# Four edits to an AdaLN, attention and LoRA-MoE kernel: rsqrt by single columns, set-up order, turned logits, order of the last downs

## What is computed

```
mod = silu(c) @ wmod -> sa, ca, ga, sb, cb, gb (one row of 256 each per batch; |ga|, |gb| at least 0.25)
h = layernorm(x) * (1 + ca) + sa
x = x + ga * (attention(layernorm(h) * gamma + beta) @ o_proj + h)      causal, one head of 256
h = layernorm(x) * (1 + cb) + sb
x = x + gb * (base FFN(h) + sum over the top 2 of 8 experts of the LoRA FFN(h) by weight)
```

## Time and profile before

| | us |
|---|---|
| runs: median (lowest to highest of 3) | 670.13 (669.81 to 670.28) |
| the profiled execution, its own time | 669.96 |
| its span, first to last instruction | 668.1 |
| busy: PE | 652.1 (98%) |
| busy: PE weight load | 561.4 (84%) |
| busy: DVE | 466.5 (70%) |
| busy: POOL | 369.5 (55%) |
| busy: ACT | 360.3 (54%) |

### The profile page before, as it was taken

One profiled execution on the slowest core, in us unless ns is written; L12 is line 12 of the kernel. 1 busy time (PEld: TensorE's weight loads), 2 busy tenths in 40 slices (PEclk: granted clock), 3 DMA queues, 4 the chain that ended last, 5 costly groups with the idle time before them and its releaser, 6 DMA issues.

```text
span 668.1 us, 10913 instructions
## 1 busy us (share of the span) xinstructions
PE 652.1 (98%) x3890; PEld 561.4 (84%) x3890; DVE 466.5 (70%) x1146; ACT 360.3 (54%) x646; POOL 369.5 (55%) x442
## 2 busy tenths in 40 slices
PE   8799999999999999999999999999999999999996
PEld 6488987888889987888889897887889998798885
DVE  5857676888785776688776677689886757547323
ACT  1766466545555547555455446564455456654543
POOL 1099366538658236657676317665666525633644
PEclk9999999999999999999999999999999999999999
DMA  8400020000000020000000001000000000000000
GB/s 308 138 1 1 2 64 0 1 1 32 0 1 32 1 65 1 0 1 33 0 1 32 1 6 59 1 1 33 1 0 27 7 1 1 1 1 1 32 0 33
DMA packets 15032, 15.47 MB, mean 23 GB/s; under 512 B 1793, under 2 KB 13697, under 8 KB 14977
## 3 DMA queue, kind: packets, MB, share of 16 engines
q1 hardware_dynamic: 14976, 14.76, 6.6%
HBM read 10.57 MB, written 4.19 MB: 22 GB/s over the span
## 4 chain that ended last, share of the span: by engine, by line
PE 84%; DVE 10%; ACT 3%; issue 1%; DMA 1%; POOL 0%; SPq 0%; DVEq 0%; ACTq 0%
PE ps L1265 78%; PE ps L1274 6%; DVE hid L1112 2%; DVE rstd L844 1%; DVE zb L864 1%; DMA xs<-in_L_attn_x 1%; DVE neg_mean L1176 1%; ACT xr L587 1%; ACT act_s L725 1%; DVE zb L867 0%; DVE stat L998 0%; DVE stat L861 0%; DVE topi L1057 0%; DVE xr L1007 0%; DVE nr_a L842 0%
## 5 line engine op out<-in xcount | busy, mean ns | idle before, releaser
L475 POOL TENSOR_TENSOR ring_lo<-hid,ring_hi 128x512 fp32r<-128x512 f32 x144 | 187.2, 1304 | 110.0 <-ACT ring_hi L733 109.4
L725 ACT ACTIVATE act_s<-ps 128x512 f32<-128x512 f32 x120 | 71.6, 597 | 123.0 <-PE ps L1265 122.4
L1112 DVE TENSOR_TENSOR hid<-act_s,ps 128x512 f32<-128x512 f32 x120 | 82.1, 684 | 78.9 <-ACT act_s L725 74.1
L733 ACT ACTIVATE ring_hi<-hid 128x512 fp32r<-128x512 f32 (+1 forms) x144 | 90.4, 627 | 5.3 <-PE ps L1265 3.5
L1265 PE MATMUL ps<-wdT_hi,ring_hi 128*128 128x256 f32 x192 | 53.2, 283 | 0.0
L1265 PE MATMUL ps<-wdT_lo,ring_hi 128*128 128x256 f32 x192 | 52.7, 280 | 0.0
L467 POOL TENSOR_TENSOR xT_lo<-tr_full,xT_hi 128x512 fp32r<-128x512 f32 x28 | 35.9, 1297 | 29.0 <-ACT xT_hi L597 29.0
L1265 PE MATMUL ps<-wdT_hi,ring_lo 128*128 128x256 f32 x160 | 44.7, 280 | 0.0
L1265 PE MATMUL ps<-vv_hi,pT_hi 128*128 128x256 f32 x144 | 42.9, 298 | 0.1
L1265 PE MATMUL ps<-tm_hi,bgT_hi 128*128 128x512 f32 x96 | 39.5, 411 | 2.4 <-DVE hid L1112 2.4
L482 POOL TENSOR_TENSOR xr<-xr,y_gb 128x256 f32<-128x256 f32 x31 | 22.6, 754 | 33.6 <-DVE y_gb L1147 33.6
(11 more groups left out here) (232 smaller groups left out, 2018.2 us busy)
## 6 DMA issues: line engine op xcount, KB each, us to landing
out<-xr SPq DMA_DIRECT2D x7, 512.0 KB, 2.9
xs<-in_L_attn_x SPq DMA_DIRECT2D x3, 1024.0 KB, 5.7
xs<-in_L_attn_x SPq DMA_DIRECT2D x2, 512.0 KB, 4.7
s_mod<-in_L_wmod SPq DMA_DIRECT2D x2, 512.0 KB, 7.6
s_qkvT<-in_L_attn_qkv SPq DMA_DIRECT2D x1, 768.0 KB, 7.4
wgT_raw<-in_L_ffn_Wg SPq DMA_DIRECT2D x1, 704.0 KB, 7.9
wuT_raw<-in_L_ffn_Wu SPq DMA_DIRECT2D x1, 640.0 KB, 8.7
wdT_raw<-in_L_ffn_Wd SPq DMA_DIRECT2D x1, 640.0 KB, 5.7
```

Of the source, the lines that this page charges most:

```text
L475: pool.tensor_sub(ring[1][:, place(n), :], hid[:, n % HID, :], ring[0][:, place(n), :].bitcast(fp32)).then_inc(h_lo.sem, 1)
L725: nc.scalar.activation(act_s[:, n % 2, :], ps[:, 2 * (n % 2), :], ACT.Silu).then_inc(silu_ready.sem, 1)
L733: nc.scalar.activation(ring[0][p0:P, place(n), :], hid[p0:P, n % HID, :], ACT.Copy).then_inc(h_hi.sem, 1)
L1112: V.tensor_mul(hid[:, n % HID, :], act_s[:, n % 2, :], ps[:, 2 * (n % 2) + 1, :]).then_inc(h_ready.sem, 1)
```

## The change

1. **Rsqrt on single columns.** For layernorm 2 of tiles 4 to 7, `guess` and `rsqrt_steps` on [128, 4] become `single_guess` and `single_steps`: four instructions of one column each, all `tensor_scalar`, with the other factors as per-partition scalars. Statistics go from r = 4 to r = 2, the guess from r = 5 to r = 3, one step each at r = 4, 5, 6.
2. **Set-up with four tiles first.** Tiles 0 to 3 of batch 0 go ahead of tiles 4 to 7 on every engine; tiles 4 to 7's transposes, queries 2, 3, all values and two gate jobs move into attention steps i = 0 to 3. Scale jobs 1 to 3 are spread from one row by `batch_rows` (four partitions) in place of a product with the weight; a third `mod_row` makes that row. 28 dummy matmuls stand ahead of the first queries. ACT runs one small Exp early. All twelve `weight_high` go to i = 2 to 6; POOL's `weight_low` 7, 8 behind the Newton steps of layernorm 2, 9 to 11 behind the two `tr_low`.
3. **Second half's logits turned.** `logits(1)` becomes `logits_across`: four matmuls with Wr as weights and 512 columns of x moving, a DVE copy of the 16x512 result at r = 12, and `logits_back`: four transposes. `router_shift(1)` comes after the x_stats of r = 12; the next batch's moments and guess at r = 13, POOL's Newton steps at r = 14 to 16. `FILL` (0, 2) goes from 2, 2, 2, 1 to 0, 4, 2, 1.
4. **Last downs.** In the last batch the base's half tile (slot 0, a = 1) is the last of the six last downs.

Beside these: the mask banks of half 0 are 6, 7 instead of 7, 6, and each mask waits for its own x1 tile; in half 1 `ln1_stats` comes before `ln1_rows`.

```diff
+        mod_rows = wmask[0:B, :, :].rearrange("p s n -> p (s n)")
+        scale_rows = y_gb[0:B, :, :].rearrange("p t d -> p (t d)")
+        batch_rows = bc[0:B, B - 1, SA:CA + 1, :]...
+        gate_spread = bc[:, :, GA:GB + 1, :]...
...
+        LAST_DOWNS = ((0, 0), (1, 0), (1, 1), (2, 0), (2, 1), (0, 1))
-        MASK_BANKS = ((7, 6, 4, 5), (3, 4, 5, 6))
+        MASK_BANKS = ((6, 7, 4, 5), (3, 4, 5, 6))
-        EARLY_HIGH = 4
-        BODY_HIGH = {0: (4, 5, 6), 1: (7,), 2: (8,), 3: (9,), 4: (10,), 5: (11,)}
+        BODY_HIGH = {2: (0, 1), 3: (2, 3, 4), 4: (5, 6, 7), 5: (8, 9, 10), 6: (11,)}
-        MOD_BANKS = (0, 1, 2, 3, 7, 2, 3, 7)
+        MOD_JOBS = (("scale", 0), ("gate", 0), ("scale", 1), ("scale", 2), ("scale", 3), ("gate", 1), ("gate", 2), ("gate", 3))
+        MOD_BANKS = (0, 2, 6, 3, 4, 2, 7, 6)
+        ROW_CHUNKS = ((0, 1), (2, 5), (3, 4))
+        FIRST_PROJ = (0, 1, 4, 5, 2, 3, 6, 7)
+        W_ROUTER, W_UP = 6, 9
... POOL
                 for it in range(NEWTON):
                     newton(b, LN2_A, 0, TC, it)
+                if b == 0:
+                    for j in range(W_ROUTER + 1, W_UP):
+                        weight_low(j)
                 for k in range(KT):
                     tr_low(b, KT * NC + k, [t[:, 0, k, :] for t in xT])
+                if b == 0:
+                    for j in range(W_UP, WEIGHT_STEPS):
+                        weight_low(j)
... ACT
+            nc.scalar.activation(lg[:, 0, :], cT[...], ACT.Exp, scale=0.0).then_inc(unwaited, 1)
                 for i in range(NT):
+                    if b == 0 and i == 0:
+                        act.wait_ge(first_shift, 2)
+                        for tile in range(TC, NT):
+                            first_normalise(tile)
... DVE
+            def single_guess(tiles):
+                for i in tiles:
+                    mark(V.tensor_scalar(nr_v[:, i:i + 1], mv[:, i, 1:2], EPS, -0.5, ALU.add, ALU.mult))
+                settle()
+                for i in tiles:
+                    mark(V.tensor_scalar(nr_i[:, i:i + 1], nr_v[:, i:i + 1].bitcast(i32), 1, None, ALU.logical_shift_right))
+                settle()
+                for i in tiles:
+                    mark(V.tensor_scalar(rstd[:, i:i + 1].bitcast(i32), nr_i[:, i:i + 1], -1.0, float(0x5f3759df + 0x40000000 - 0x00400000), ALU.mult, ALU.add))
+                settle()
+            def single_steps(tiles):
+                for i in tiles:
+                    y = rstd[:, i:i + 1]
+                    mark(V.tensor_scalar(nr_a[:, i:i + 1], y, y, nr_v[:, i:i + 1], ALU.mult, ALU.mult))
+                settle()
+                for i in tiles:
+                    y = rstd[:, i:i + 1]
+                    mark(V.tensor_scalar(y, nr_a[:, i:i + 1], 1.5, y, ALU.add, ALU.mult))
+                settle()
...
-                    if r == 4:
+                    if r == 2:
                         x1_stats(TC + 3)
                         moments(range(TC, NT))
-                    if r == 5:
-                        mark(V.tensor_scalar(neg_mean[:, TC:NT], mv[:, TC:NT, 0], -1.0, None, ALU.mult))
-                        link(guess(TC, TC))
-                        rsqrt_steps(TC, TC, range(NEWTON - 1))
+                    if r == 3:
+                        single_guess(range(TC, NT))
+                    if 4 <= r < 4 + NEWTON:
+                        single_steps(range(TC, NT))
...
                     if r == 12:
-                        router_shift(1)
+                        dve.wait_ge(logits_wide.sem, logits_wide.at(b, 0))
+                        V.tensor_copy(logit_rows, ps[0:2 * E, LOGIT_BANK[1], :]).then_inc(logits_copied.sem, 1)
...
+                        if 3 <= r < 3 + NT:
+                            ln1_stats(r - 3)
                         if 2 <= r < 2 + NT:
                             ln1_rows(b + 1, r - 2)
-                        if 3 <= r < 3 + NT:
-                            ln1_stats(r - 3)
... PE, set-up
-                if what == "scale":
+                if job == 0:
                     for k in range(KT):
                         last_mm = mm(ps[:, bank, :], s_scb[:, k, b, :], s_mod[:, k, 0:2 * D], k == 0, k == KT - 1)
+                elif what == "scale":
+                    last_mm = mm(ps[:, bank, :], batch_rows[:, b, :], scale_rows, True, True)
...
+            attention_transposes(0, 0, [xr[:, i, :] for i in range(TC)])
+            mod_turned(1, modT_ready)
+            modulation(3)
+            pe.wait_ge(product_lo, 1)
+            modulation(4)
+            pe.wait_ge(mod_copied, 2)
+            for _ in range(28):
+                mm(ps[:, 2, 0:P], identb[:, :], identb[:, :], True, True)
+            queries(0, (0, 1))
+            pe.wait_ge(gates_spread, 2)
+            modulation(5)
... PE, attention of batch 0
+                        if b == 0 and i == 0:
+                            values(b, range(NT // 2))
+                        if b == 0 and i == 1:
+                            attention_transposes(b, 1, [xr[:, t, :] for t in range(TC, NT)])
+                            pe.wait_ge(modT_copied, 1)
+                            modulation(6)
+                            modulation(7)
+                        if b == 0 and i == 3:
+                            values(b, range(NT // 2, NT))
...
+                    if b == 0 and i == 2:
+                        queries(b, (2, 3))
... PE, FFN
+                def logits_across(ci):
+                    pe.wait_ge(tr_lo.sem, tr_lo.at(b, KT * NC + ci * KT + 1))
+                    o = ps[0:2 * E, LOGIT_BANK[ci], :]
+                    for k in range(KT):
+                        x_hi, x_lo = inputs(ci)[k]
+                        mm(o, wr_both[:, k, :, :].rearrange("p h e -> p (h e)"), x_hi, k == 0, False)
+                        last_mm = mm(o[0:E, :], wr_both[:, k, 0, :], x_lo, False, k == KT - 1)
+                    last_mm.then_inc(logits_wide.sem, 1)
+                def logits_back(ci):
+                    pe.wait_ge(logits_copied.sem, logits_copied.at(b, 0))
+                    for t in range(TC):
+                        last = transpose(ps[:, LOGIT_BANK[ci], 2 * t * E:2 * (t + 1) * E], logit_rows[:, t * P:(t + 1) * P], ident[0:2 * E, 0:2 * E])
+                    last.then_inc(logits_ready.sem, 1)
...
-                pe.wait_ge(x1_ready.sem, x1_ready.at(b, NT - 1))
                 for m in range(2):
+                    pe.wait_ge(x1_ready.sem, x1_ready.at(b, NT - 2 + m))
                     pe.wait_ge(masks_spread.sem, masks_spread.at(b, 0))
                     mask(0, m)
...
-                for d, f in enumerate(last_downs(1)):
+                for d, f in enumerate([(1, GROUPS - 1, s, a) for s, a in LAST_DOWNS] if last else last_downs(1)):
```

More of the change, by code:

```diff
@@ L503, in _ @@
                 residual(0, i)
-            for j in range(WEIGHT_STEPS):
+            for j in range(W_ROUTER + 1):
                 weight_low(j)
@@ L567, in _ @@
             nc.scalar.activation(scT[:, :, :], cT[:, :, :], ACT.Silu).then_inc(sc_ready, 1)
+            nc.scalar.activation(lg[:, 0, :], cT[:, :, :].rearrange("p k b -> p (k b)"), ACT.Exp, scale=0.0).then_inc(unwaited, 1)
             def modulation(job):
@@ L940, in _ @@
             moments(range(NT))
-            rsqrt(0, NT)
+            mark(guess(0, NT))
+            settle()
+            for n, small in enumerate(first_newton(0, NT)):
+                mark(small())
+                at = steps[1]
+                if n == TC:
+                    dve.wait_ge(first_scale, 1)
+                if TC <= n < 2 * TC:
+                    ln1_centre(0, n - TC)
+                dve.wait_ge(vstep, at)
             dve.wait_ge(mod_copied, 1)
-            for i in first:
-                ln1_centre(0, i)
             settle()
@@ L958, in _ @@
             mark(guess(0, TC, True))
-            big = [lambda i=i: ln1_centre(0, i) for i in second] + [lambda i=i: first_rows(i) for i in second] + [wqk_low]
+            g = gateT[:, :]
+            clamps = {3: (lambda: V.tensor_copy(g, ps[:, TURN_BANK, 0:2 * KT * B]),),
+                      4: (lambda: V.tensor_scalar(gate_sign[:, :], g, 0.0, 2.0, ALU.is_ge, ALU.mult),
+                          lambda: V.scalar_tensor_tensor(gate_size[:, :], g, -1.0, g, ALU.mult, ALU.max)),
+                      5: (lambda: V.tensor_scalar_max(gate_size[:, :], gate_size[:, :], 0.25),)}
             settle()
@@ L1015, in body @@
                         V.tensor_reduce(rowmax[:, i:i + 1], banks[:, 0:w], X, ALU.max, negate=True).then_inc(rowmax_ready.sem, 1)
+                    if b == 0 and i == 0:
+                        queries_values(b, (4,))
+                    if b == 0 and i == 1:
+                        attention_scale(b, range(KT, KT * NC))
+                        for q in range(KT, KT * NC):
+                            attention_low(q)
+                        queries_values(b, (5,))
+                    if b == 0 and i == 3:
+                        queries_values(b, (6, 7))
```

(25 more changed lines are left out.)

246 lines of the change are left out of this document (145 added, 101 removed).

## The result

| | kernel before | changed kernel |
|---|---|---|
| median of the runs | 670.2 us (6; 669.8 to 670.9) | 665.5 us (6; 664.7 to 667.7) |
| ratio, 95% interval | | 0.993 (0.992 to 0.994) |
| the profiled execution: its time, its span | 669.96, 668.1 | 664.67, 662.9 |

What follows compares the result with a forecast made beforehand. TensorE, busy for 98% of the span, was taken as the bound, so time could come only from its waits or work. Terms summed to -5.45 on the profiled 669.96, giving 664.5; the median, 0.17 above, gave 664.6; range 660 to 669.5.

Steps and rivals of the forecast that it cites:

- steady terms: Gains outside the set-up and batch 0's router; the time from one batch's router to the next falls by about 1.25 us.
- Rival A: Layernorm 2's guess: one-column instructions do wait for POOL, base 2.8 us late, +2.05 a batch, 674.6, slower; chance 0.12.
- Rival B: Batch 0's router: POOL's late low parts don't meet it and the set-up gets its full gain, 661.9; chance 0.27.
- D: Set-up and router moves cancel wholly and the small ones are hidden anyway, 669 to 671; chance 0.05.
- C: Set-up: the clock falls in the new gap at 42, or the chain is as much longer: +1.5 to +3, 666.6; chance 0.18.
- Set-up, -2.05: Batch 0's set-up up to the first probs transpose of i = 4: queries start at 29.4 against 34.89, gain 2.05 us.
- Weights late, +1.5: Batch 0's router: POOL's low parts 9 to 11 delay Vector's router instructions and then the masks, 1.5 us lost.
- Single columns, -1.85: Layernorm 2's rsqrt, four batches: one-column instructions ignore POOL, 0.75 us wait goes, base waits 0.3; net -0.46 a batch.
- Logits turned, -1.4: Second half's logits, four batches: 16 matmuls of 1.70 us become 0.91 plus at most 0.44, -0.35 each.
- Masks, -0.6: Masks of three batches: bank 6 first needs x1 of tile 6 only, tile 7 0.22 us later, -0.2 each.
- Statistics first, -0.75: Second half, three batches: with statistics ahead of rows, 0.13 to 0.37 us of the 0.37 wait at unit 4 goes.
- Last downs, -0.3: End of the last batch: the half tile covers 0.9 us, but the last adapter down waits for its stacked half, -0.3.

Runs made afterwards that it cites:

- e1: The kernel before with all later parts of the change applied and its old set-up left alone: 664.9 us, ratio 0.992.
- e4: Changed kernel with POOL's low part 9 ahead of batch 0's two tr_low, 10 behind them, 11 waiting until the masks are spread: 664.4 us, ratio 0.991.
- e3: Changed kernel without the 28 dummy matmuls ahead of the first queries: 665.9 us, ratio 0.994.
- e7: As e4, with 30 dummies spread: 14 behind the first transposes, 8 between the narrow jobs, 8 ahead of the queries: 662.5 us, ratio 0.989.
- e2: Changed kernel with layernorm 2's rsqrt for the second tiles on four columns at once, at its old units: 667.2 us, ratio 0.995.
- e11: Changed kernel with the three groups of the guess each as one instruction on four columns, steps still on single columns: 672.3 us, ratio 1.003.
- e5: Changed kernel with the second half's logits not turned, as in the kernel before: 667.0 us, ratio 0.996.
- e6: Changed kernel with mask banks and their wait, statistics before rows, and the order of the last downs undone: 668.8 us, ratio 0.997.
- e8: As e4, with GpSimd's residuals from tile 3 on waiting for Vector's low parts of the second tiles: 663.5 us, ratio 0.990.
- e10: The changed kernel run once more, unaltered, beside the kernel before: 665.8 us, ratio 0.993.
- e12: Changed kernel with each group of the guess as one instruction on three columns and one on a single column: 673.5 us, executed once.

## Why the prediction was right, and where it was not

664.6 was forecast and 665.5 measured; on the profiled executions, a gain of 5.45 forecast and 669.96 - 664.67 = 5.29 measured. (The sum as it stands gives 664.68 for the median, not 664.6; and the first product came 0.31 later in the changed execution, so from there the spans differ by 5.5.) The steady terms came as forecast, and rivals A and B did not. Of D, the first half came: set-up and router cancel but for 0.1 (e1); the second, that the small ones are hidden, did not. C's fall of the clock in the gap at 42 did not come either (the clock stays at 1.00 there); a fall came 15 us earlier instead. Term by term:

- **Set-up, -2.05.** Measured at its own anchor, from the first product: 57.20 - 10.07 less 56.30 - 10.38 is 1.21. e4 beside e1 gives 1.18 at the masks. The step that failed is the one that said that the 28 dummies "end at 28.8, so they cost nothing and cover the gap in which the clock fell". They ran from 27.59 to 30.55, most of it at half clock, because the clock had fallen before them, and the queries, which without them start 1.5 earlier (e3), waited for them. e7 shows the price: with the dummies spread and the clock at 1.00, 1.51 more comes. (That makes 2.7 over the kernel before, more than the 2.05: the other steps were taken some 0.6 too dear.) The rest of the chain stood: ACT done at 23.57 (forecast 23.3), 0.96 of wait at the scores (0.9), 2.11 ahead of t = 1 (2.0).
- **Weights late, +1.5.** The mechanism was right, the size 0.4 too large: e4 takes away 1.1. L1156 was 1.0 longer, not 1.8, since it started 0.7 into adT_lo and not at its start, and L1150 0.2 longer. Rival B, that it would not be met, fell, and even with the collision taken away (e4, 664.4) its 661.9 does not come, since its other half was the set-up's full gain. By the sum of the two terms -0.55 was forecast; -0.1 came (e1).
- **Single columns, -1.85.** e2: 1.7 by the medians, 1.56 by the stretches between the masks. Instruction by instruction it was less exact: the groups of the guess took 0.37 (forecast 0.44), a step 1.45 (forecast 0.9), because the instructions of a step take 0.27 and 0.20 each, not 0.08. The cover, base's 2.7 us a unit, was wide enough. That base would wait 0.3 at unit 6: 0.14. Rival A's condition is refuted: no column waits. Its price was too high: base 2.8 late was forecast, and with the guess in the form that waits it is 1.76 late, 1.62 more than in the changed kernel (e11; 672.3 in all, where 674.6 was forecast).
  By the Trainium skill's VectorE: DVE Perf Modes, Mode 2×_2P, even counts, and odd ones that are equal in source and destination, take both ports. Four columns and three agree with it (1.22 beside GpSimd's instruction); one column, which was read in the prediction as odd and equal, does not behave so (0.144).
- **Logits turned, -1.4.** e5: 1.35 by the stretches between the masks; per place 0.43 for 0.35, less 0.18 given back by the wait at 296.59 in three batches.
- **Masks, -0.6.** 0.2 in each of three batches (e6), and 0.3 in batch 0, which was forecast as slack.
- **Statistics first, -0.75.** The wait of 0.37 at 310.94 is 0.04 now: 0.33 a batch, 1.0 in all, near the upper bound of 0.37. Undone in the changed kernel it costs 0.58 (e6), with a second instruction that comes to wait for GpSimd.
- **Last downs, -0.3.** 0.35 (e6), and by the step named: ACT's stacked half at 653.13 holds the last adapter down until 653.81.

The steady terms came to 4.9 in the forecast; 3.6 + 1.5 is measured in the batches. The period was to fall by about 1.25: it fell by 1.09, 1.32 and 1.22, and the places give it again: 0.42 + 0.25 + 0.21 + 0.33 = 1.21. So does the last batch: 0.56 + 0.59 + 0.35 = 1.5, from e2, e5 and e6. The forecast is thus right for the reasons given in the batches. In the set-up the number is right in part by luck: two errors there (0.85 too much gain, 0.4 too much loss) partly cancel.

What stays open: why the clock falls in a stretch that counts as busy, and which of the two new groups of dummies in e7 keeps it.

## What to carry to other kernels

Where small statistics sit between large instructions and GpSimd works in SBUF all the time, write them on single columns: twelve instructions that never wait were worth 6.5 us against three that do. Before work is moved to fill one engine's idle time, look at what runs on the other of the pair Vector and GpSimd at the new time: a move that was worth 1.2 us was given back by three low parts of weights that had slid into the router. And if a set-up's clock falls, look when it falls, and try fillers ahead of that time, not only in the last gap ahead of the real work: some thirty small matmuls were worth nothing measurable in one place (e3) and 1.5 us in the other (e7).

## What the runs showed of the hardware beyond that

- A TENSOR_SCALAR of one column (L912) took 0.14 us at all of its 16 places, each time with a GpSimd instruction running; with three or four columns it took 1.2 where GpSimd's had just started, and 0.17 between two of them (four columns, e11). One column with both scalar operands read from SBUF columns (L925) took 0.27, with one such operand (L929) 0.20.
- The granted clock fell with TensorE counted as busy (at 26.8 in the changed kernel; between 26.2 and 28.7 in e2 to e6, e8 and e10 to e12), and stayed down 3.4 us or 6.8 us, differently from one execution to the next of the same code up to there. It goes with the time: of the changed kernel's eleven executions the five with a mean granted clock of 0.997 took 664.7 to 665.3, the five with 0.995 took 665.7 to 666.2, and the one with 0.991 took 667.7. Executions at 0.991 or 0.990 (two of e5, 669.2) have less clock than a stretch of 6.8 us accounts for (the profiled ones with it have 0.994 or 0.995); no trace of one was kept.
- The first product started anywhere between 10.07 and 11.35 us. In all profiled executions but e12's it starts 0.05 or 0.06 behind the start of the last of the 110 warm-up dummies, so it waited for nothing else. The dummies run first at some 12 a microsecond and then at some 22; in the kernel before the pace changes between 5 and 6 us, in e1 between 8 and 9, and the granted clock reads 1.00 in both.
